# A second weight buffer for the second feed-forward product of the six inner layers

## The reference

```python
def ffn_layer(x, g, bln, W1, b1, W2, b2):        # x: 2048 x 1024, shifted tokens
    mu = x.mean(-1, keepdims=True)
    var = ((x - mu) ** 2).mean(-1, keepdims=True)
    xn = (x - mu) / jnp.sqrt(var + 1e-05) * g + bln
    hg = xn @ W1 + b1                            # W1: 1024 x 5460
    a, gate = jnp.split(hg, 2, -1)               # 2730 columns each
    return a * jax.nn.gelu(gate, approximate=False) @ W2 + b2   # W2: 2730 x 1024
for i in range(DEPTH):                           # DEPTH = 6
    x = attn_layer(shift_tokens(x), ...) + x
    x = ffn_layer(shift_tokens(x), ...) + x
```

## Time and profile before

| | |
|---|---|
| median of three runs | 28257.48 us |
| the profiled execution | 28266.21 us |
| its span, slowest core (core 5) | 28264.7 us |
| spans of the eight cores | 28160.7 to 28264.7 us |
| mean granted TensorE clock | 0.641 to 0.643 |
| PE busy | 13569.5 us, 48% |
| DVE, ACT, POOL busy | 22%, 21%, 18% |
| software DMA queue, share of 16 engines | 21.9%, 619.45 MB |
| HBM read | 1179.31 MB |

### The profile page before, as it was taken

One profiled execution on the slowest core, in us unless ns is written; L12 is line 12 of the kernel. 1 busy time (PEld: TensorE's weight loads), 2 busy tenths in 40 slices (PEclk: granted clock), 3 DMA queues, 4 the chain that ended last, 5 costly groups with the idle time before them and its releaser, 6 DMA issues.

```text
span 28264.7 us, 164760 instructions; the slowest of 8 cores (28160.7 to 28264.7 us)
## 1 busy us (share of the span) xinstructions
PE 13569.5 (48%) x53460; PEld 4928.8 (17%) x53460; DVE 6276.3 (22%) x5402; ACT 6042.0 (21%) x7952; POOL 5009.5 (18%) x5430
## 2 busy tenths in 40 slices
PE   4553255551555523655425555155553355534445
PEld 1111022220222201222102222011221122211112
DVE  2221421005220033210142100422002421022222
ACT  2542011230112221122201122111222111212222
POOL 1002222112221122221222211222112222110000
PEclk8776557775567765577755677555776557765555
DMA  2003003540015520044300255000452003430001
GB/s 48 1 10 47 10 0 31 47 48 14 1 15 46 47 28 6 3 41 47 39 11 0 26 47 50 16 2 9 45 46 33 8 1 36 46 67 3 3 3 19
DMA packets 2215199, 705.91 MB, mean 25 GB/s; under 512 B 2164832, under 2 KB 2177408, under 8 KB 2207200
## 3 DMA queue, kind: packets, MB, share of 16 engines
q0 software_dynamic: 2190784, 619.45, 21.9%
q1 hardware_dynamic: 23584, 75.92, 0.7%
HBM read 1179.31 MB, written 33.55 MB: 43 GB/s over the span
## 4 chain that ended last, share of the span: by engine, by line
PE 38%; DVE 17%; ACT 15%; POOL 12%; DMA 9%; issue 8%; another core or an unknown queue 1%; ACTq 1%; DVEq 0%; POOLq 0%; SPq 0%
PE i_psCtx L270 16%; PE i_psX L270 12%; ACT L186 6%; DVE i_psCtx L186 5%; POOL i_eT L186 5%; DMA i_arW<-in_w 4%; POOL i_q L186 4%; PE i_psD L270 3%; DMA i_arW<-in_wqkv 3%; PE f_psS L270 3%; DVE i_mcols L186 2%; DVE f_mxc L186 2%; PE f_psC L270 2%; ACT f_eT L186 2%; ACT a_eAB L186 2%
## 5 line engine op out<-in xcount | busy, mean ns | idle before, releaser
L186 ACT ACT_TABLE_LOAD x1967 | 2523.7, 1283 | 15505.3 <-PE i_psCtx L270 7746.2
L270 PE MATMUL i_psCtx<-i_arK,i_arW 128*128 128x512 bf16 (+1 forms) x8448 | 2837.0, 511 | 1780.7 <-ACT i_stb L186 1780.7
L258 POOL DMA_DIRECT2D i_arW<-in_w x1440 | 1295.9, 905 | 7221.1 <-PE i_psCtx L270 4450.1
L270 PE MATMUL i_psX<-i_arV,i_arW 128*128 128x512 bf16 (+1 forms) x4224 | 1401.2, 503 | 1638.8 <-DMA i_arW<-in_w 1578.5
L270 PE MATMUL i_psCtx<-i_eT,i_arV 128*64 128x128 bf16 x4320 | 1341.5, 311 | 1663.2 <-POOL i_eT L186 1663.2
L186 POOL TENSOR_TENSOR i_eT<-i_eT,i_m_s 128x384 bf16<-128x384 bf16 (+2 forms) x1536 | 1324.3, 862 | 3538.6 <-ACT i_eT L186 3426.3
L186 DVE RECIPROCAL i_psD<-i_psD 2x512 f32<-2x512 f32 x192 | 644.7, 3358 | 4402.8 <-PE i_psD L270 4383.7
L270 PEld LDWEIGHTS i_psCtx<-i_arK,i_arW 128*128 128x128 bf16 (+1 forms) x8448 | 1019.8, 125 | 3432.5 <-issue 3124.9
L186 ACT ACTIVATE i_eT<-i_psX 128x384 bf16<-128x384 f32 (+2 forms) x1536 | 724.9, 472 | 3927.6 <-PE i_psX L270 3916.1
L186 DVE SCALAR_TENSOR_TENSOR i_arV<-i_psCtx,i_b1a_s,i_arV 128x512 bf16<-128x512 f32 (+1 forms) x528 | 396.1, 750 | 5125.7 <-ACT i_arV L186 5125.7
L270 PE MATMUL i_psX<-i_zbt,i_arW 128*128 128x512 bf16 x3072 | 991.4, 486 | 886.6 <-DMA i_arW<-in_wqkv 831.6
(11 more groups left out here) (245 smaller groups left out, 16715.0 us busy)
## 6 DMA issues: line engine op xcount, KB each, us to landing
i_arW<-in_w POOLq DMA_DIRECT2D x1008, 256.0 KB, 4.9
i_arW<-in_w POOLq DMA_DIRECT2D x192, 672.0 KB, 7.1
i_arW<-in_wqkv POOLq DMA_DIRECT2D x384, 256.0 KB, 4.6
i_q<-i_arA POOLq DMA_DIRECT2D x192, 128.0 KB, 2.7
i_q<-i_arK POOLq DMA_DIRECT2D x192, 128.0 KB, 2.7
i_arW<-in_wqkv POOLq DMA_DIRECT2D x12, 1024.0 KB, 10.6
i_arW<-in_rot POOLq DMA_DIRECT2D x24, 512.0 KB, 6.1
i_arW<-in_wo POOLq DMA_DIRECT2D x48, 256.0 KB, 4.5
```

The source lines that it names most:

```text
L186: inst = f(*a, **kw)
L258: return self.ec.inc(sem, self.r.dma_start(out=out, in_=in_), 16)
L270: inst = self.r.matmul(out, lhsT, rhs, start=start, stop=stop, skip_group_check=skip)
```

## The change

The w2 weights get a second place, columns 12288 to 15104 of arV, which the hidden tile and the GELU scratch (columns up to 12288) leave free. Even chunks use the old place, odd ones the new one, each with a semaphore of its own. The load of chunk `widx` now waits for the products of chunk `widx - 2`; the first two of a layer wait for the last w1 step of the first quarter. The wait of the first w1 load of a quarter for the last w2 chunk is gone; what is left in front of it is the wait that every w1 load has.

No instruction is added, taken out or moved in any queue. On GpSimd the rows of two w2 chunks of one quarter read as follows before; each pair is one chunk's load.

```diff
--- before.py
+++ after.py
@@ -1191,8 +1191,8 @@
         laug = rows3[0:2, 0:N]
 
         for sname in ("ldz", "ldc", "ldk", "ldw", "ldwA", "ldwB", "ldt",
-                      "lds", "ldw1A", "ldw1B", "ldw2", "ldwoA", "ldwoB",
-                      "st0"):
+                      "lds", "ldw1A", "ldw1B", "ldw2A", "ldw2B", "ldwoA",
+                      "ldwoB", "st0"):
             ec.sem(sname)
         tok = {}
         for _li in range(nlayers):
@@ -1982,7 +1982,11 @@
             return arW[:, pp * 2048 + half * 1024:
                        pp * 2048 + half * 1024 + 1024]
 
-        w2b = arW[:, 4096:4096 + 2816]
+        w2bA = arW[:, 4096:4096 + 2816]
+        w2bB = arV[:, 12288:12288 + 2816]
+
+        def w2buf(widx):
+            return w2bA if widx % 2 == 0 else w2bB
 
         for qtr in range(4):
             def g_zb3(g, qtr=qtr):
@@ -2017,8 +2021,6 @@
                     G = GW(ec, g)
                     if idx == 0:
                         G.wait("cPE", wo_p0 + 32)
-                    if qtr > 0 and jp == 0:
-                        G.wait("cPE", tok[("w2c", qtr * NDK - 1)])
                     if idx >= 2:
                         G.wait("cPE", tok[("w1c", idx - 2)])
                     sname = "ldw1A" if pp == 0 else "ldw1B"
@@ -2116,15 +2118,17 @@
 
                 def g_w2(g, qtr=qtr, oc=oc, widx=widx):
                     G = GW(ec, g)
-                    if widx >= 1:
-                        G.wait("cPE", tok[("w2c", widx - 1)])
+                    if widx >= 2:
+                        G.wait("cPE", tok[("w2c", widx - 2)])
                     else:
                         G.wait("cPE", tok[("w1c", NJP - 1)])
-                    G.dma("ldw2", w2b[:, 0:21 * 128],
+                    w2b = w2buf(widx)
+                    sname = "ldw2A" if widx % 2 == 0 else "ldw2B"
+                    G.dma(sname, w2b[:, 0:21 * 128],
                           bass.AP(w2_h.tensor, w2_h.offset + oc * 128,
                                   [[D, 128], [128 * D, 21], [1, 128]]))
                     tok[("w2l", widx)] = G.dma(
-                        "ldw2", w2b[0:42, 21 * 128:21 * 128 + 128],
+                        sname, w2b[0:42, 21 * 128:21 * 128 + 128],
                         bass.AP(w2_h.tensor,
                                 w2_h.offset + 2688 * D + oc * 128,
                                 [[D, 42], [1, 128]]))
@@ -2132,10 +2136,12 @@
 
                 def t_w2(t, qtr=qtr, oc=oc, widx=widx):
                     T = TW(ec, t)
-                    T.wait("ldw2", tok[("w2l", widx)])
+                    T.wait("ldw2A" if widx % 2 == 0 else "ldw2B",
+                           tok[("w2l", widx)])
                     T.wait("cDVE", tok[("hst", qtr * NJP + NJP - 1)])
                     if widx >= 2:
                         T.wait("cDVE", tok[("zu2", widx - 2)])
+                    w2b = w2buf(widx)
                     bank = psX[:, (widx % 2) * 512:(widx % 2) * 512 + 512]
                     for ik in range(NJP):
                         kw = JW[ik]
```

## The result

The changed kernel takes 26888.88 us (median of 8 runs, 26825.01 to 26921.23) against 28255.25 us before (8 runs, 28222.97 to 28349.93). The ratio is 0.951, 95% interval 0.9496 to 0.9524. The forecast was 26775 us with a range of 26590 to 26990 us: the direction, the mechanism and the range hold, the point is 114 us too low. The profiled execution took 26825.08 us, 1441 us less than that of before; 1481 us were forecast for this difference. It is one of the fastest of the changed kernel.

What follows compares the result with a forecast made beforehand. W2 products and their weight loads take turns, with TensorE waiting. Per quarter 4 x 6.7 + 5.0 + 3 x 9.5 = 60.3 us, 1481 us saved, giving 26775 us; range 26590 to 26990 us.

Steps and rivals of the forecast that it cites:

- The waits of the loads: The w2 product's waits for its load fall from 174 to about 78, from 1578.5 to about 376 us.
- L: W2 stage: from the end of products that free a place to the start of those using it; 9.5 us.
- rival 2: Loads of the eight cores disturb one another: every L 12.4 us, 69 us per quarter, 26985 us; chance 0.11.
- M2: Time of the 22 matmuls of a pair's second w2 chunk, following without a gap: 5.0 us.
- rival 3: Clock lower under dense load on all cores: M2 7.0 us, M1 7.3, 26882 us; chance 0.04.
- M1: Time of the 22 matmuls of a pair's first w2 chunk, after about 4.5 us of rest: 6.7 us.
- The sum: W2 stage per quarter: 4 M1 + M2 + 3 L = 60.3 us; 24 take 1447 us.
- From the profile to the median: The median of the runs lies 9 us below the profiled execution: 26785 us becomes 26775 us.
- Parts costed at nothing: Second place, casts, w1 wait (at most 7 us), layers' first loads, last quarter (9 us): set against each other at zero.
- rival 1: Clock stays up through the rest between pairs: M1 5.0 us, 53.5 us per quarter, 26613 us; chance 0.10.
- the slower outcome (4): Two loads in flight per core slow shared memory; at L 33 us the time is 28468 us; chance 0.03.
- no overlap (5): A wait elsewhere in GpSimd's queue holds every load until the product before has ended: 28257 us; chance 0.02.

Runs made afterwards that it cites:

- the other parts alone: Kernel before with only the first w1 load's wait removed: 1.0018; changed kernel with its second place but the old waits: 1.0.
- half a load: Kernel before with 11 of the 21 full tiles of each w2 load, used twice by the products: 27862.03 us, 0.9835.
- three places: Changed kernel with three places for w2 weights, each load waiting for the chunk three before: 26566.38 us, 0.9391 of the kernel before.
- six: Changed kernel with six places for w2 weights, four of them in arK: 26410.35 us, 0.9338 of the kernel before.
- two places and old waits: Changed kernel, each w2 load again waiting for the chunk before and the first w1 load for the last w2 chunk: 28298.65 us, 1.0.
- the w1 wait gone alone: Kernel before, a quarter's first w1 load no longer waiting for the last w2 chunk: 28343.39 us, 1.0018.

## Why the prediction was right, and where it was off

- **The waits of the loads.** Right in place, count and size: 75 waits for 78, 361 us for 376. The loads come in pairs nearly everywhere. Odd chunks waited 10 times. In 6 of these the first chunk ahead took about as long as a second at the same clock, so it covered nothing beyond (layer 3 above); in the other 4 the load itself came later. The three waits missing from the 78 would each have stood behind such a wait. Asking earlier is what earns it; the other parts alone earn nothing that the time shows.
- **L, 9.5 us.** Read from the trace as the time from the end of chunk 0, 2 or 4 to the start of chunk 2, 4 or 6, it is 9.62 us in the mean of 72, where a load before took 9.1. In the last quarter of all it is 15.4 us after 11.4 before; elsewhere it is 9.4 after 9.0. So rival 2 (12.4 us) did not come, but in the one quarter from which it took its number it would have been too mild. The working behind L was off: the least wait, 8.6 us there, is 8.64 us in the earlier trace rows but 8.36 in the trace, and latency is 2.5 us of the 7.1, not nearly half, as half a load shows.
- **M2, 5.0 us.** The term that failed in kind. It is 5.01 to 5.03 us wherever the chunk follows at once and the clock is 1.00, but 5.28 in the mean (5.04 to 5.28 on the eight cores): half of the excess is the granted clock of 0.81, the other half the five second chunks that had to wait themselves and ran in part at 1.2 GHz. The first half is rival 3 in kind, to which I gave 0.04, though far from its size of 7.0 us; both together cost 24 x 0.28 = 7 us. Against it I had one stretch of 20 us in which three cores of a die were busy and had 1.00. One stretch early in the program could not carry that: in the same profile core 3 had 0.81 in the output projection of layer 4, as shown above, and core 5, whose trace is the one read there, in parts of its w1 stages, where TensorE is busy about half of the time (13234.5 to 13240.5, for one). The Trainium skill ("TensorE: Matmul & The Clock Gate", Part 1) gives 13/16, that is 0.81, for sustained dense matmuls on three or more cores of a die. The measured level agrees with it; that three busy cores always bring it does not, by the earlier trace rows, as far as the times of several cores, each counted from its own start, can be laid side by side.
- **M1, 6.7 us.** It is 681.8 / 96 = 7.10 us, the term that was furthest off: 24 x 4 x 0.4 = 38 us. The estimate of 1.7 us over a dense product came from 16 matmuls after 6.3 us of rest in another stage. Here 22 matmuls took 6.31 to 7.95 us after rests of 3.7 to 5.9 us (once 5.01, after 3.67), and up to 8.29 us where the chunk began at 1.2 GHz and ended at 0.81.
- **The sum.** 4 x 7.10 + 5.28 + 3 x 9.62 = 62.5 us per quarter instead of 60.3. The 24 w2 stages of the trace take 1508.8 us, 62.9 each, after 2928.0 us before; 1447 were forecast, 62 us fewer. Of these M1 makes 38, L 9 and M2 7; the rest is mostly waits of last chunks, which the sum does not have. The profiled execution is only 40 us above the forecast for it, since the rest of the program took 25314.7 us instead of 25336.6. Of these 22 us the shorter borders explain 7; the cause of the other 15 is open; executions of one kernel differ by more (26825.01 to 26921.23).
- **From the profile to the median.** I took the median to lie 9 us below the profiled execution, as before. It lies 64 us above. The runs of the changed kernel differ by what clock the cores were granted: in the run of 26825.01 us the cores had 0.645 to 0.649, in that of 26921.23 us one die had 0.637 to 0.639. So 40 of the 114 us are the sum, M1 above all, and 73 are this step: the execution that was profiled lay low among its like. Of the nine executions the longer ones had the lower clock on their slowest core, from 0.645 at 26825.01 us down to 0.633 at 26913.58 (0.638 at 26921.23), which speaks for the clock but does not separate it from other causes. All three terms and this step erred the same way, so only the 22 us outside the w2 stages made the forecast look better than its terms.
- **Parts costed at nothing.** The w1 wait: 1.0018 in the time, and the 7 us that the prediction gave as the most it could bring, by the borders. The border: 11.24 us remain. GpSimd's casts: hidden, they end 2.5 to 7.5 us before the eighth product does. The last quarter: costed at 9 us for three waits and set against others; its L of 15.4 us makes 18.
- **Rivals.** The clock that stays up (rival 1) came for 5 of the 96 first chunks, at 5.01 or 5.03 us after rests of at most 3.67 us, and the disturbed loads (2) for the last quarter; the slower outcome (4) and no overlap (5) did not come.

## What to carry to other kernels

A second buffer does not divide a wait by two: with a load of L from the end of the product that frees its place, and products of M, the waits left are about L - M for every second product, and none once the products between request and use add up to L. Ask for that number first; here three places were enough (some 43 us of waits left) and two were not. Price the matmuls on both sides of a wait too, since a rest brings the clock down, and allow for a granted clock of 0.81 in part of the time. Before one stretch at 1.00 is taken as proof against it, look at all cores and all layers of the trace at hand: here it was in the trace of the kernel before.

## What the runs showed of the chip that I had not expected

- A granted clock of 0.81, in stretches of tens of us (60 us in one output projection; in another on the same core the product took 69.44 us in place of 57.04), beside 1.00 for the same work in other stretches. How much of it there is does not follow from how dense the kernel is. On the slowest core of one profile each it was 674 us before, 788 in the change, 1958 with three places, 779 with six, and 2637 us with two places and old waits, which is as sparse as the kernel before. It differs between the dies of one execution: with the w1 wait gone alone, 48 to 142 us on the four cores of one die and 1339 to 1672 on those of the other. What brings it about no run here shows.
- The time of a run goes with the mean clock that its cores were granted. With two places and old waits, ten runs went from 28194.42 us at a mean of 0.644 to 28364.04 us at 0.631.
- Work that nobody needs made the kernel faster by 1.1%: 5712 matmuls in the gaps.
